# Biases turned on TensorE, three blocks of x summed by VectorE, three h0 units abreast

## The reference

```
# x: (32, 64, 512), cond: (32, 256), all float32
q  = relu(cond @ W3 + b3)                                # (32, 512)
x1 = (64 * x + sum of x over its 64 rows) * q            # per batch
h0 = relu(x1 @ W2 + b2)                                  # (32, 64, 512)
w1, w2 = ternary(W_fc), ternary(W_proj)                  # sign, or 0, times a scale for 64 weights
h  = relu(h0 @ w1.T) ** 2                                # (32, 64, 2048)
hn = h * rsqrt(mean(h ** 2) + eps)
out = x + hn @ w2.T                                      # (32, 64, 512)
```

## Time and profile before

| | us |
|---|---|
| median of 3 runs | 311.33 |
| the profiled execution | 311.55 |
| its span in the profile | 309.8 |
| PE busy | 304.8 |
| DVE / ACT / POOL busy | 188.4 / 191.3 / 114.9 |
| span until the first h0 matmul | 11.48 |
| h0 units, with the turning of groups 1 to 3 | 11.48 to 71.91 |

### The profile page before, as it was taken

How to read it: one execution, slowest core, us unless ns; L and a number is a source line. 1 busy time by engine, 2 the same in 40 slices (tenths; PEclk the granted TensorE clock), 3 DMA queues, 4 the chain that set the end, 5 groups by cost and what they waited for, 6 DMA issues and landing times.

```text
span 309.8 us, 3790 instructions
## 1 busy us (share of the span) xinstructions
PE 304.8 (98%) x1278; PEld 232.9 (75%) x1278; DVE 188.4 (61%) x310; ACT 191.3 (62%) x282; POOL 114.9 (37%) x106
## 2 busy tenths in 40 slices
PE   8999999999999999999999999999999999999994
PEld 8654545447888888888888888888888888888883
DVE  0679999996888778886257335952233483222335
ACT  1682666697999599976746444555554445555540
POOL 1035586645433323335333331253333314333330
PEclk9999999999999999999999999999999999999999
DMA  6994644342654043113004200340000033000003
GB/s 213 353 338 153 212 128 105 102 123 81 179 163 102 1 102 37 34 34 68 2 0 177 95 0 1 135 139 0 0 0 2 0 135 138 0 0 0 2 1 138
DMA packets 31332, 27.03 MB, mean 87 GB/s; under 512 B 18736, under 2 KB 20816, under 8 KB 31312
## 3 DMA queue, kind: packets, MB, share of 16 engines
q1 hardware_dynamic: 29936, 26.22, 28.5%
q10 hardware_dynamic: 1376, 0.56, 0.7%
HBM read 18.39 MB, written 4.19 MB: 73 GB/s over the span
## 4 chain that ended last, share of the span: by engine, by line
PE 95%; DVE 2%; ACT 1%; issue 1%; DVEq 0%
PE ps_acc L366 37%; PE ps_out L378 35%; PE ps_acc L350 18%; PE ps_out L337 2%; PE ps_out L328 1%; PE ps_acc L421 1%; DVE x_sb L580 1%; PE ps_x L435 1%; ACT x_t L673 0%; ACT x_t L670 0%; ACT wv_sb L676 0%; DVE y_hi L523 0%; DVE x_t L510 0%; DVE y_lo L525 0%; DVEq L113 0%
## 5 line engine op out<-in xcount | busy, mean ns | idle before, releaser
L261 POOL TENSOR_TENSOR wv_sb<-wv_sb 128x512 f32<-128x512 f32 x55 | 71.8, 1306 | 121.9 <-DVE y_lo L525 114.8
L378 PE MATMUL ps_out<-w_t,y_hi 128*128 128x512 f32 x256 | 100.1, 391 | 0.0
L366 PE MATMUL ps_acc<-h_hi,w_t 128*128 128x512 f32 x256 | 100.0, 391 | 0.0
L378 PE MATMUL ps_out<-w_t,y_lo 128*128 128x512 f32 x256 | 99.6, 389 | 0.0
L366 PE MATMUL ps_acc<-h_lo,w_t 128*128 128x512 f32 x256 | 99.6, 389 | 0.0
L523 DVE CAST y_hi<-x_t 128x512 fp32r<-128x512 f32 x64 | 33.0, 516 | 86.2 <-PE ps_out L378 71.6
L670 ACT ACTIVATE x_t<-ps_acc 128x512 f32<-128x512 f32 x64 | 37.9, 592 | 62.0 <-PE ps_acc L366 62.0
L350 PE MATMUL ps_acc<-x_t,wv_sb 128*128 128x512 f32 x128 | 56.3, 593 | 0.3 <-DVE x_t L510 0.3
L366 PEld LDWEIGHTS ps_acc<-h_lo,w_t 128*128 128x128 f32 x256 | 48.1, 188 | 10.2 <-issue 0.2
L366 PEld LDWEIGHTS ps_acc<-h_hi,w_t 128*128 128x128 f32 x256 | 48.1, 188 | 10.2 <-ACT h_f L665 0.2
L378 PEld LDWEIGHTS ps_out<-w_t,y_hi 128*128 128x128 f32 x256 | 48.1, 188 | 10.1 <-DVE y_lo L525 0.3
(11 more groups left out here) (57 smaller groups left out, 171.3 us busy)
## 6 DMA issues: line engine op xcount, KB each, us to landing
x_sb<-in_x_dram SPq DMA_DIRECT2D x5, 1024.0 KB, 5.7
raw<-in_L_ffn_W_fc_dram SPq DMA_DIRECT2D x8, 512.0 KB, 6.4
raw<-in_L_ffn_W_proj_dram SPq DMA_DIRECT2D x8, 512.0 KB, 4.3
out_dram<-x_sb SPq DMA_DIRECT2D x16, 256.0 KB, 2.1
x_odd<-in_x_dram SPq DMA_DIRECT2D x2, 1024.0 KB, 7.5
x_sb<-in_x_dram SPq DMA_DIRECT2D x4, 256.0 KB, 4.7
wv_sb<-in_L_cond_W_dram SPq DMA_DIRECT2D x4, 256.0 KB, 8.6
x_t<-in_L_cond_W_dram ACTq DMA_DIRECT2D x1, 512.0 KB, 5.0
```

The costliest lines, as they stand in the source:

```text
L261: engine.tensor_tensor(acc, acc, y_sq[:, v % SQ_RING, :], ALU.add).then_inc(sq_added, 1)
L366: last = pe.matmul(ps_acc[:, (UNITS + v) % ACC_RING, :], w_t[:, j, k * P:(k + 1) * P], part[:, k, g * BANK:(g + 1) * BANK], start=(k == 0 ...
L378: last = pe.matmul(ps_out[:, t, :], part[:, v % RING, t * P:(t + 1) * P], w, start=(opens(v) and part is y_hi), stop=(closes(v) and part i ...
```

## The change

Four edits. First, the biases are loaded as eight rows of 128 (512 bytes each) onto eight partitions, turned by one PE transpose into a spare corner of `ps_acc`, and copied by DVE to `bias_t`; the transpose stands on PE between x part 1 and q, ACT's q waits for the copy. Second, of group 0 only block 0 still goes through `sum_mat`; blocks 1 to 3 are turned (one pass for each part instead of two) and DVE forms the sum; the factor q is applied by DVE itself for block 1, by POOL for blocks 2 and 3. Third, units 0, 1 and 2 run abreast (`make_h0_abreast`): for each k the three matmuls of the units, and the 16 transposes of group 1 stand ahead of the last k. DVE and POOL therefore do the sums of group 1 before they round units 0 and 1, and within group 0 the sums stand ahead of the rounding. Fourth, SP loads the W2 columns 0, 1 and 2 ahead of the first pair, and x of group 2 ahead of the first DMA transpose.

```diff
-    SUMS_OF_UNIT = [[[], [], [0, 1, 2, 3], []], [[0], [1], [2, 3], []], [[0], [1], [2, 3], []]]
+    SUMS_OF_UNIT = [[[], [0, 1, 2, 3], [], []], [[0], [1], [2, 3], []], [[0], [1], [2, 3], []]]
+    ABREAST = ACC_RING
     def sums_by_vector(g, k):
-        return g > 0
+        return g > 0 or k > 0
+    def scaled_by_pool(g, k):
+        return g > 0 or k > 1
...
+        bias_sb = h0_f[0:2 * KD, 0, Q:Q + P]
+        bq_t = bias_t[:, 0:KD]
+        bv_t = bias_t[:, KD:2 * KD]
...
             load_wv(0)
+            load_wv(1)
+            load_wv(2)
             load_pair(0)
-            load_wv(1)
             load_pair(1)
-            load_wv(2)
             load_pair(2)
...
-                turn_pair(i)
                 if i == 0:
                     load_x(2)
+                turn_pair(i)
...
+            def make_h0_abreast():
+                for k in range(KD):
+                    if k == KD - 1:
+                        for b in range(KD):
+                            turn_x(1, b)
+                    for u in range(ABREAST):
+                        if k == 0:
+                            pe.wait_ge(wv_loaded[u], 16)
+                        if u == 0:
+                            pe.wait_ge(*x1_made(0, k))
+                        last = pe.matmul(ps_acc[:, u, :], wv_sb[:, k, u * P:(u + 1) * P], x1_t[:, 0, k, :],
+                                         start=(k == 0), stop=(k == KD - 1))
+                        if k == KD - 1:
+                            last.then_inc(h0_done, 1)
...
+                    pe.wait_ge(biases_loaded, 32)
+                    pe.transpose(ps_acc[:, 0, KQ * BATCHES:KQ * BATCHES + 2 * KD], bias_sb,
+                                 ident_f[0:2 * KD, 0:2 * KD]).then_inc(biases_turned, 1)
...
-                    last = sum_x_block(0, t, k)
+                    if sums_by_vector(0, k):
+                        last = pe.transpose(ps_out[:, k, t * P:(t + 1) * P], x_sb[:, t, k * P:(k + 1) * P], ident_f[:])
+                    else:
+                        last = sum_x_block(0, t, k)
...
-            for u in range(UNITS):
+            make_h0_abreast()
+            for u in range(ABREAST, UNITS):
...
@@ DVE, in scale_x, after the reduce and the scaled add
-                    return
+                    if scaled_by_pool(g, k):
+                        return
+                    dve.wait_ge(x1_added, at + 1)
+                    src = x1
...
@@ DVE, the loop over the units
+            dve.wait_ge(biases_turned, 1)
+            dve.tensor_copy(bias_t[:], ps_acc[:, 0, KQ * BATCHES:KQ * BATCHES + 2 * KD]).then_inc(biases_ready, 1)
...
-                if u > 0:
+                if g > 0:
                     round_h0(u - 1)
                 if g + 1 < GROUPS:
                     for k in SUMS_OF_UNIT[g][m]:
                         scale_x(g + 1, k)
+                if g == 0 and u > 0:
+                    round_h0(u - 1)
                 if u in STEP_AT_UNIT:
                     step(STEP_AT_UNIT[u])
...
@@ ACT
-            act.dma_start(bq_t[:], b_q.rearrange("(m p) -> p m", p=P), allow_slow_non_contiguous=True).then_inc(bq_loaded, 16)
-            act.dma_start(bv_t[:], b_v.rearrange("(m p) -> p m", p=P), allow_slow_non_contiguous=True).then_inc(bv_loaded, 16)
+            act.dma_start(bias_sb[0:KD, :], b_q.rearrange("(m p) -> m p", p=P)).then_inc(biases_loaded, 16)
+            act.dma_start(bias_sb[KD:2 * KD, :], b_v.rearrange("(m p) -> m p", p=P)).then_inc(biases_loaded, 16)
...
@@ POOL
+            for k in range(KD):
+                if scaled_by_pool(0, k):
+                    times_q(0, k)
             for u in range(UNITS):
-                if u > 0:
+                g, m = u // KD, u % KD
+                if g > 0:
                     rest_of_h0(u - 1)
...
+                if g == 0 and u > 0:
+                    rest_of_h0(u - 1)
```

More of the change, by code:

```diff
@@ L93, in adaln_ffn @@
     STEP_AT_TILE = {1: 8, 3: 9, 5: 10, 10: 11, 12: 12, 14: 13, 16: 14, 18: 15}
-    SUMS_OF_UNIT = [[[], [], [0, 1, 2, 3], []], [[0], [1], [2, 3], []], [[0], [1], [2, 3], []]]
+    SUMS_OF_UNIT = [[[], [0, 1, 2, 3], [], []], [[0], [1], [2, 3], []], [[0], [1], [2, 3], []]]
+    ABREAST = ACC_RING
     def sums_by_vector(g, k):
-        return g > 0
+        return g > 0 or k > 0
     def added_before(g, k):
         return len([1 for a in range(g + 1) for b in range(KD if a < g else k) if sums_by_vector(a, b)])
+    def scaled_by_pool(g, k):
+        return g > 0 or k > 1
     def scaled_before(g, k):
-        return KD * g + k - added_before(g, k)
+        blocks = [(a, b) for a in range(g + 1) for b in range(KD if a < g else k)]
+        return len([1 for a, b in blocks if scaled_by_pool(a, b) == scaled_by_pool(g, k)])
     KEEP_AT_TILE = {19: 14, 20: 15}
@@ L146, in adaln_ffn @@
         ones = sb("ones", [P, 1], F32)
-        bq_t = sb("bq_t", [P, KD], F32)
-        bv_t = sb("bv_t", [P, KD], F32)
+        bias_t = sb("bias_t", [P, 2 * KD], F32)
         abs_sum = sb("abs_sum", [P, SG], F32)
@@ L184, in adaln_ffn @@
         wq_loaded = sem("wq_loaded")
-        bq_loaded = sem("bq_loaded")
-        bv_loaded = sem("bv_loaded")
+        biases_loaded = sem("biases_loaded")
+        biases_turned = sem("biases_turned")
+        biases_ready = sem("biases_ready")
         wv_loaded = [sem(f"wv_loaded{i}") for i in range(KD)]
@@ L241, in x1_made @@
         def x1_made(g, k):
-            return (x1_scaled, added_before(g, k) + 1) if sums_by_vector(g, k) else (x1_ready, scaled_before(g, k) + 1)
+            return x1_scaled if scaled_by_pool(g, k) else x1_ready, scaled_before(g, k) + 1
         def x_read(g, k):
@@ L683, in _ @@
             act.dma_start(wq_sb[:], w_q.rearrange("(k p) d -> p k d", p=P)).then_inc(wq_loaded, 16)
-            act.dma_start(bq_t[:], b_q.rearrange("(m p) -> p m", p=P), allow_slow_non_contiguous=True).then_inc(bq_loaded, 16)
-            act.dma_start(bv_t[:], b_v.rearrange("(m p) -> p m", p=P), allow_slow_non_contiguous=True).then_inc(bv_loaded, 16)
+            act.dma_start(bias_sb[0:KD, :], b_q.rearrange("(m p) -> m p", p=P)).then_inc(biases_loaded, 16)
+            act.dma_start(bias_sb[KD:2 * KD, :], b_v.rearrange("(m p) -> m p", p=P)).then_inc(biases_loaded, 16)
             act.wait_ge(consts_ready, 1)
             act.activation(root[:, 0:1], ones[:], ACT.Sqrt)
-            act.wait_ge(bq_loaded, 16)
+            act.wait_ge(biases_ready, 1)
             act.wait_ge(q_done, 1)
@@ L695, in _ @@
             spread_pair(0)
-            act.wait_ge(bv_loaded, 16)
             for u in range(UNITS):
@@ L743, in _ @@
                                pattern=[[-1, P]], channel_multiplier=1).then_inc(consts_ready, 1)
+            for k in range(KD):
+                if scaled_by_pool(0, k):
+                    times_q(0, k)
             for u in range(UNITS):
-                if u > 0:
+                g, m = u // KD, u % KD
+                if g > 0:
                     rest_of_h0(u - 1)
-                g, m = u // KD, u % KD
                 if g + 1 < GROUPS:
                     for k in SUMS_OF_UNIT[g][m]:
-                        if sums_by_vector(g + 1, k):
-                            times_q(g + 1, k)
+                        times_q(g + 1, k)
+                if g == 0 and u > 0:
+                    rest_of_h0(u - 1)
             rest_of_h0(UNITS - 1)
```

## The result

The changed kernel took 312.28 us in the median of 22 executions (311.75 to 314.62), the kernel before on the same chip 311.32 (22 executions, 311.15 to 311.81). The ratio is 1.0047, 95% interval 1.0035 to 1.0058: slower, by 1.0 us in the median and 1.5 in the mean, by which the ratio goes. The median hides two groups: 12 executions lie at 311.75 to 312.45 (about 312.0), ten at 313.38 to 314.62 (about 313.7). The kernel before has one group. The mean granted clock of each execution parts them as well: 0.993 to 1.0 in the lower group, 0.986 to 0.989 in the upper.

What follows compares the result with a forecast made beforehand. PE, busy 98% of the span, was taken as the bound; -0.9 at the start, +1.4 waiting at unit 5 and +0.1 after gave +0.6 on 311.33, so 311.9 us, range 310.3 to 313.6.

Steps and rivals of the forecast that it cites:

- Ahead of the first h0 matmul: PE's start: fewer passes bring the first h0 matmul to 10.58, 0.9 us sooner, after about 0.9 us idle.
- X: Time of the DVE instruction making the first x1: forecast 9.75, where it was 10.65 before.
- x1 abreast, columns, x of group 1 and 2: Inputs of the first units: each ready before PE needs it, no wait; x1 blocks at worst 0.2 us each.
- DVE behind it: DVE after group 0's sums: starts group 1's sums at 20.2 against 21.71, fourth scaled add at 25.5.
- The main step, the lock at L510: Before unit 5: POOL's subtraction holds the shared ports, delaying DVE's small instruction and ACT's relu; PE waits 1.4 us.
- Rival 1: At that small DVE instruction the lock falls to DVE; PE waits only 0.4 us at unit 5; 310.9 us, chance 0.17.
- rival 2: No wait at unit 5, so the gain at the start stays; 310.4 us, chance 0.18.
- The sum: Whole kernel: -0.9 at the start, +1.4 wait at unit 5, +0.1 behind it, giving +0.6 us.
- rival 3: PE's faster pass rate comes later, q's passes stay 0.21 apart; 313.5 us; chance 0.27 together with rival 4.
- rival 4: The eight bias rows land late and hold q back, up to 1 us more; chance 0.27 together with rival 3.

Runs made afterwards that it cites:

- after_again: The changed kernel run again without any edit; 312.34 us, ratio 1.0045 to the kernel before.
- in_sequence: `relu_first_plain` with units 0 to 2 one after another instead of abreast; 314.27 us, ratio 1.0090 to the kernel before.
- late_columns: `relu_first_plain` with W2 columns 1 and 2 loaded behind a pair each, as in the kernel before; 311.23 us, ratio 0.9995.
- relu_first: `scale_first` with ACT's relu of unit 3 also moved ahead of the steps that wait for DVE; median 311.07 us, ratio 1.0013.
- scale_first: Changed kernel with DVE's sum_pair(2) ahead of the two CASTs of units 0 and 1; median 313.25 us, ratio 1.0048.
- all_turns: Changed kernel with 12 transposes of the identity as warm-up instead of 6 matmuls; 312.10 us, ratio 1.0036.
- plain_turn: Changed kernel with blocks 1 to 3 of x parts 0 and 1 turned by two-pass identity matmuls instead of transposes; 312.35 us, ratio 1.0029.
- relu_first_plain: `relu_first` with blocks 1 to 3 of x parts 0 and 1 turned by plain identity matmuls instead of transposes; 311.19 us, ratio 0.9997.
- bias_after_q: `relu_first_plain` with the transpose of the biases behind q's matmuls instead of ahead; 310.81 us, ratio 0.9980.
- biases_only: Kernel before with the first edit alone, biases loaded as rows, turned on PE, copied by DVE; 311.20 us, ratio 0.9989.
- warm_turns: Kernel before with 12 transposes of the identity as warm-up instead of seven matmuls of zeros; 311.38 us, ratio 0.9997.
- warm_plain: Kernel before with six matmuls of the identity as warm-up instead of seven matmuls of zeros; 311.48 us, ratio 1.0005.

## Why the prediction was right, and where it was not

**Ahead of the first h0 matmul** (forecast 10.58, with 0.9 us idle; came 10.63 and 0.62). The parts took 6.73 - 4.38 = 2.35 instead of the 2.30 worked out, q started at 6.86 (6.81), X was 9.80 (9.75). The idle time was named too long: part 3's last pass ended at 10.01, and by my own terms (8.56, nine distances of 0.11, a latency of 0.27) PE would have run dry at 9.8, not 9.7, and idled 0.8. The profile with an early rise (`after_again`) comes to nearly the same, 10.59, by another way: PE waits for the biases.

**x1 abreast, columns, x of group 1 and 2:** no wait, as said. That this depends on running abreast, `in_sequence` showed; `late_columns` shows no price for later columns, as far as it goes. The prediction gave x of group 1 no time; it lands at 17.0, 1.3 us sooner than before, and is needed at 18.43.

**DVE behind it:** group 1's sums at 20.25 (20.2), the fourth scaled add at 25.53 (25.5), each within 0.1.

**The main step, the lock at L510,** held in all its parts: CAST of unit 1 behind POOL's product, POOL's second subtraction from 28.82 and L510 from 28.90 (a margin of 0.08, forecast 0.07, so a near thing), L510 for 1.21 us, relu of unit 2 done at 31.78 (31.7), PE at 31.83 (31.9). Without it unit 5 would have started at 10.63 + 19.87 = 30.50 (`relu_first` has just this distance, 10.66 to 30.53), so the delay is 1.33 against 1.4; the row's 1.17 is less because it is counted from the end of the last transpose. `scale_first` took the cause away and the wait went. The rows of `scale_first` show the same for DVE's bf16 tensor_tensor with both inputs in SBUF (L517, L520: 1.75 and 1.64 instead of 0.69). The Trainium skill, SBUF — State Buffer, Who interferes with whom, has the exclusive lock of DVE and POOL for casts and tensor_scalar, and says that a tensor_tensor with both inputs in SBUF contends with POOL's reads; the rows of L510, the CASTs, L517 and L520 agree. Rival 1 had the lock fall to DVE, and rival 2 no wait: both fell.

**The sum** was -0.9 + 1.4 + 0.1 = +0.6; measured to the first hidden matmul -0.85 + 1.33 + 0.15 = +0.63, where the first two make the 0.48 by which unit 5 starts later. The end gives back 0.1 by the last pass and some 0.3 behind it, which I had not taken up. The lower group's 312.0 lies 0.1 over the forecast of 311.9.

**What it left out:** I wrote of rival 3, a late rise of the pass rate, as something that happens or doesn't, with a chance of 0.27 for it and rival 4, and put none of it in the forecast. Something of its size happens in some executions of the same kernel: ten of 22. They move the median from 312.0 to 312.28 and the mean ratio further. So the forecast of 311.9 names the lower group well and the kernel's median only nearly, and that with luck: with 12 of 22 in the upper group the median would have been 313.4.

What ties the upper group to TensorE's clock is the mean granted clock of its executions, 0.986 to 0.989, where the others have 0.992 or more. Whether it is rival 3 is another matter. In the kept profiles a late rise leaves no mark in this number: it reads 1.00 in the first microseconds too, where the passes stand 0.21 apart, and `late_columns`, profiled with a late rise, has a mean of 1.0. Its low stretch in `after_again` (mean 0.998) stands at the very end, behind PE's last pass (view of stretches, the clock is the third number from the end):

```profile
2.00:3.00 1.00, 1.00 (x6) 1.00 (x6) 0.00 (x0) 0.40 (x1) 0.36 (x2) 1.00 0.77 264
...
308.00:309.00 1.00, 0.00 (x0) 0.00 (x0) 0.00 (x0) 0.00 (x0) 0.00 (x0) 0.82 0.69 258
309.00:310.00 1.00, 0.00 (x0) 0.00 (x0) 0.00 (x0) 0.00 (x0) 0.00 (x0) 0.50 0.01 2
```

So a clock that had risen and fell again for a while would fit the upper group's low mean at least as well as one that rose late, and the execution of 314.79 at 0.997 is the one that looks like a late rise alone. Neither is shown. What in the kernel brings the group on, the experiments show only as a count. I take a clock of 0.995 or less as the mark, which is wider than the upper group:

| parts 0 and 1 of x | kernels | executions | of these at 0.995 or less |
|---|---|---|---|
| transposes | changed (twice), `scale_first`, `relu_first`, `all_turns` | 65 | 29 |
| matmuls against the identity | `plain_turn`, `relu_first_plain`, `bias_after_q`, `in_sequence`, `late_columns` | 44 | 1 |
| matmuls against sum_mat | `biases_only`, `warm_turns`, `warm_plain` | 30 | 0 |

So the low clock comes, but for one execution, only with what stands in parts 0 and 1 of the changed kernel, ten passes with six transposes among them, and replacing the transposes by two-pass matmuls ends the upper group. Whether it is the kind of the passes or their number is open. The warm-up seems to have a part too: a clock of 0.989 or less is found in 23 of 55 executions with the matmuls of zeros and in none of the 10 with transposes (`all_turns`). The one at 0.993 is of `in_sequence`, the kernel in which PE idles most. The Trainium skill, TensorE: Matmul & The Clock Gate, Part 4: PE-mode transpose, says that transposes don't count as activity for the clock. By that `all_turns` should have been late nearly always, and it wasn't. Open remain when the clock was low in an execution of the upper group and how the 1.7 us come about, since none was caught in a profile; that q's passes stand 0.21 apart there, as rival 3 has it, is not shown. A mean of 0.988 means half the clock (1.2 instead of 2.4 GHz) for 2.4% of some 311 us, 7.5 us, if the records are taken at their word. By my estimate that would cost 3.7 us where PE's queue is unbroken, so at most about half of it can lie there.

**Rival 4,** late biases: they come at about 6.6 (7.2 in the profile of `in_sequence`). In the profiled execution PE arrived just then; in those in which the rate rises early it stood 0.3 to 0.7 us for them (0.72 in the second profile of the changed kernel), and `bias_after_q` gained 0.4 us over `relu_first_plain` (310.81 against 311.19). I had priced it as 0 to 1 and put it at 0; the forecast's own execution agreed, the early ones didn't.

## What to carry to other kernels

Work moved to another engine must be followed by its neighbours in time, not only by its length: here 0.85 us won at the start were lost again by one 0.17 us instruction that met a subtraction on POOL, and moving it alone only handed the wait to the next unit. Look at the spread of the executions before the median: with two groups, the median tells which is larger, and an edit is judged group by group. Order what PE waits for by when it lands: q's weights were there before the bias rows, and letting q go first was worth 0.4 us. Before blaming one cause for a group of longer executions, catch one in a profile: here a count of executions shows which edit ends them, and not what happens in them.

## What the runs showed of the hardware

The moment at which PE's passes go from 0.21 to 0.11 us apart differs between executions of the same instructions by over 2 us. `relu_first_plain` and `late_columns` have the same PE program; the first has its two passes against `sum_mat` in 0.49 us, from 4.21, and its six identity passes of part 0 in 0.83, the second in 0.80 and 1.49, with the fast rate only from about 6.5:

```profile
4.21 0.49 PE L340 MATMUL ps_out<-sum_mat,x_sb 128*128 128x128 f32 x2
4.53 0.83 PE L471 MATMUL ps_out<-ident_f,x_sb 128*128 128x128 f32 x6
...
10.54 7.96 PE L364 MATMUL ps_acc<-x_t,wv_sb 128*128 128x512 f32 x18 [0.62 <-DVE x_t L550]
```

The first h0 matmul is 0.77 us apart (10.54 and 11.31), and the two executions 0.84 (310.83 and 311.67). That is about the width of the groups in most kernels here, and a reason not to read a difference of under 1 us at the start from one profile of each kernel.
